# Attention on TensorE: the turning products of the older odd tile moved up behind the even tile's logits

## The chip, the cores and the metric

The kernel runs on one core of one Trainium2 chip. The metric is the device time of one execution in microseconds (us); the time before is the median of three executions. One further execution was profiled, and all rows below come from it.

## The reference, cut to what matters

Input x is 4 x 1024 x 256. Three stages follow one another: a half feed-forward stage, attention, and a half feed-forward stage again. The change touches attention alone, which for each of 4 batches and 16 heads computes

```
dots = einsum('bhid,bhjd->bhij', l2norm(q), l2norm(k)) * 10      # 1024 queries, 1024 + 4 keys
dots = einsum('hg,bgij->bhij', W_pre_th, dots)                   # heads mixed
dots = where(causal, -max, dots)
dots = where(dots < 64th largest of the row, -max, dots)
attn = softmax(dots)
attn = einsum('hg,bgij->bhij', W_post_th, attn)                  # heads mixed again
out  = einsum('bhij,bhjd->bhid', attn, v) * head_scale
x    = x + (out * sigmoid(x @ Wg + bg)) @ Wo
```

## The kernel before

**Tiles, steps, blocks.** Attention works on tiles g of 8 query rows x 16 heads = 128 partitions. There are NT = 512 tiles, 128 for each batch, and they are processed in pairs: step k takes the tiles 2k (even) and 2k+1 (odd), so there are S = 256 steps. Eight steps are a block of 128 query rows. Block ib (0 to 7) of a batch has up to 4 + 128 (ib+1) keys to look at, so all vector work of a tile grows with ib, and the costs of a step too.

**Each engine has its own list of instructions, written out by hand as a loop over k.** The engines meet only at semaphores, and an engine that waits holds up all that stands behind it in its list. What belongs to one tile is spread over several steps (the tile's age is k minus its own step):

- TensorE `units(G, slots[i])`: raw scores of the *next* block, in units of two matmuls (two heads) into banks 0 and 1. There is one pair of banks, so each unit first waits for VectorE's copy of the unit before it (`s_sb`). VectorE's `scored` (line 1372, Sn) copies them out, and a DMA stores them. A step of the first six of a block has four places for units, `slots[0]` to `slots[3]`. Where the next block needs 8 units (and in the last block of all, which has none) `slots[0]` is always empty; with 16 units (blocks 2 to 5) `slots[0]` holds one unit in the steps k%8 = 1, 2, 4, 5; with 24 (block 6) in k%8 = 0 to 5. That makes 22 steps per batch and 88 in all.
- TensorE `mix(g, ..)` (lines 1020, 1024): the mixed logits of tile g, of age 0. VectorE's `take` (line 1383, D) brings them to SBUF. After the odd take GpSimd computes a first guess of the threshold (line 1217, nt), and ScalarE counts against it (line 1142), four rounds over the next steps. TensorE puts two tiny matmuls (lines 1033, 1034) of an older pair behind the odd mix; VectorE reads them as a flag (line 1379) ahead of the odd take.
- VectorE `sides` (line 1397, W), `closest` (1404), `picked` (1412) and `select` (1462, E) find the exact threshold and apply it. `sides` needs GpSimd's line 1252.
- TensorE `post(g)` (line 1047): the **turning products**. One product for each 128 keys turns the probabilities E to keys x (heads, rows) and mixes the heads on the way (its moving operand is kr, line 1285 of GpSimd). Up to four chunks share a bank, two banks take turns, and with more than four chunks a tile has two groups. Even tiles are turned at age 4 at the end of a step, odd tiles at age 5. ScalarE's `turned` (line 1165, AT) evicts them, and a group waits for the eviction of the group two before it (`at`).
- TensorE `values(hb, part)` (lines 1075, 1080): the product with V for 64 query rows, in four parts: part 0 at k%4 = 0, parts 1 and 2 at k%4 = 1, part 3 at k%4 = 2. Part 0 waits for the evictions of its eight tiles. So 64 steps, two in each block (k%8 = 1 and 5), hold part 1; here they are called values steps.

**Order in a step.** VectorE: even take, scored(slots[0]), sides x2, flag, odd take, scored(slots[1]), closest x2, threshold, picked, scored(slots[2]), even select, gated, scored(slots[3]), odd select. ScalarE: last count x2, even turned, second count x2, even exps, odd turned, odd exps, third count x2, first count x2. For values steps TensorE has: even mix, values part 1, unit, odd turning products, odd mix, unit, values part 2, unit, even turning products, unit.

Of the kernel before, what the change touches and what calls it, by code (L numbers as in the profile page):

```python
# [720 lines left out]
S = NT // 2  # L721
# [25 lines left out]
def mix_plan(g):  # L747

    cuts = mix_cuts(g)
    if len(cuts) == 1:  # L750
        return [(0, g % 3)]
    if len(cuts) == 2:
        return [(1, 2), (0, 1)] if g % 2 else [(0, 0), (1, 1)]
    return list(enumerate(range(3)))


def turn_groups(g):

    ib, t = g // TPB % IB, g % TPB
    chunks = list(range(ib + 2 if t == TPB - 1 else ib + 1))  # L760
    return [chunks[i:i + 4] for i in range(0, len(chunks), 4)]
# [12 lines left out]
def unit_slots(G):  # L774

    total = len(score_units(G))
    used = 16 if total <= HP else UNITS
    return [range(total * min(i, used) // used, total * min(i + 1, used) // used) for i in range(UNITS)]
# [5 lines left out]
                post=1, at=1, av=1, ut=1, y=1, x_ok=1, link=1, chain=1, general=1)  # L784


def attention(nc, banks, mkT, kT_all, tail, qd, kd, gd, vd, x1d, x2d, sd, mix_rows, mem_v, Wo_d, delta_c,
# [16 lines left out]
    for G in range(NB):  # L804
        UC.append(UC[-1] + (len(score_units(G)) if G else 0))

    USED = [bank for g in range(NT) for _, bank in mix_plan(g)]
    LAST = [max([j for j in range(max(0, m - 4), m) if USED[j] == USED[m]], default=-1) for m in range(MC[NT])]

    def last_use(m):  # L810

        return LAST[m]

    def searched(p):

        return 0 <= p < S and 2 * p % (IB * TPB) >= FIRST
# [8 lines left out]
    with ExitStack() as ctx:  # L825
# [167 lines left out]
        def _(pe):  # L993
            def units(G, us):
                for u in us:
                    i = UC[G] + u
                    p, (c0, c1) = score_units(G)[u]
                    if u == 0:
                        pe.wait_ge(s["k_in"][G % 2], 16 * (G // 2 + 1))
                        if G == 1:  # L1000
                            pe.wait_ge(s["k_in"][0], 16)
                        pe.wait_ge(s["q_in"], 16 * G)
                        pe.wait_ge(s["kmean"], G + 1)
                    if i >= 1:
                        pe.wait_ge(s["s_sb"], i)
                    nc.tensor.matmul(ps[0][:, 0:c1 - c0], qT[0:DH, p, :], kT[0:DH, p, c0:c1], start=True, stop=True)  # L1006
                    nc.tensor.matmul(ps[1][:, 0:c1 - c0], qT[DH:P, p, :], kT[DH:P, p, c0:c1], start=True,  # L1007
                                     stop=True).then_inc(s["s_ps"], 1)

            def mix(g, p):  # L1010
                pe.wait_ge(s["sg_in"][g % 3], 16 * (g // 3 + 1))
                for i, (k, v) in enumerate(mix_plan(g)):
                    c0, c1 = MP[g][k]
                    m, c, bank = MC[g] + i, c1 - c0, ps[2 + v]
                    diagonal = k == len(MP[g]) - 1
                    if last_use(m) >= 0:
                        pe.wait_ge(s["taken"], TAKE[last_use(m)])
                    if last_use(m) in FLAGGED:
                        pe.wait_ge(s["flag"], FLAGGED[last_use(m)])
                    out = nc.tensor.matmul(bank[:, 0:c], kpre[:].rearrange("p h r -> p (h r)"), Sg[:, g % 3, c0:c1],  # L1020
                                           start=True, stop=not diagonal)
                    if diagonal:
                        pad = len(MP[g]) == 2
                        out = nc.tensor.matmul(bank[:, c - R8 - pad:c], deltab[:], maskb[:, 0:R8 + pad], start=False,  # L1024
                                               stop=True)
                    if m in FLAGGED:
                        out = missed(p, bank)
                    out.then_inc(s["mixed"], 1)

            def missed(p, bank):  # L1030
                e = 2 * p % 8
                pe.wait_ge(s["bad"], FP[p] + 1)
                nc.tensor.matmul(bank[:, HELD:HELD + 1], onesb[:], bad[:, e:e + 1], start=True, stop=False)
                return nc.tensor.matmul(bank[:, HELD:HELD + 1], onesb[:], bad[:, e + 1:e + 2], start=False,
                                        stop=True)

            def post(g):
                pe.wait_ge(s["prob"], g + 1)
                pe.wait_ge(s["kr"], g + 1)
                ib = g // TPB % IB  # L1040
                for j, chunks in enumerate(turn_groups(g)):
                    i = PC[g] + j
                    if i >= 2:
                        pe.wait_ge(s["at"], i - 1)
                    for c in chunks:
                        rows = P if c <= ib else MEM
                        out = nc.tensor.matmul(ps[5 + i % 2][0:rows, c % 4 * P:(c % 4 + 1) * P],  # L1047
                                               E[:, g % 4, c * P:c * P + rows], kr[:, g % 4, :], start=True, stop=True)
                    out.then_inc(s["post"], 1)
# [36 lines left out]
            def project(G):  # L1086
                pe.wait_ge(s["ut"], UT[2 * (G + 1)])
                for p in range(HP):
                    out = nc.tensor.matmul(ps[7][:, 0:DIM], gT[:, p, :], Wo[:, p, :], start=(p == 0),
                                           stop=(p == HP - 1))  # L1090
                out.then_inc(s["y"], 1)
# [3 lines left out]
            for k in range(S + 16):  # L1095
                G = k // 8 + 1
                slots = [range(0)] * 4
                if G < NB and k % 8 < UNITS // 4:
                    slots = unit_slots(G)[4 * (k % 8):4 * (k % 8) + 4]
                if k < S:  # L1100
                    mix(2 * k, k - 3)
                if k >= 9 and (k - 9) % 4 == 0 and (k - 9) // 4 < 2 * NB:
                    values((k - 9) // 4, 1)
                units(G, slots[0])
                if 0 <= k - 5 < S:
                    post(2 * (k - 5) + 1)
                if k < S:
                    mix(2 * k + 1, k - 3)
                elif searched(k - 3):
                    if k == S:  # L1110
                        pe.wait_ge(s["taken"], TC[NT])
                    else:
                        pe.wait_ge(s["flag"], FP[k - 3])
                    missed(k - 3, ps[2]).then_inc(s["mixed"], 1)
                units(G, slots[1])
                if k >= 10 and (k - 10) % 4 == 0 and (k - 10) // 4 < 2 * NB:
                    values((k - 10) // 4, 3)
                if k >= 9 and (k - 9) % 4 == 0 and (k - 9) // 4 < 2 * NB:
                    values((k - 9) // 4, 2)
                if k >= 8 and (k - 8) % 4 == 0 and (k - 8) // 4 < 2 * NB:  # L1120
                    values((k - 8) // 4, 0)
                units(G, slots[2])
                if k >= 15 and (k - 15) % 8 == 0 and (k - 15) // 8 < NB:
                    project((k - 15) // 8)
                if 0 <= k - 4 < S:
                    post(2 * (k - 4))
                units(G, slots[3])
# [708 lines left out]
```

## Time and profile before

| | |
|---|---|
| median of 3 executions | 3582.88 us (3573.04 to 3583.82) |
| the profiled execution | 3581.46 us |
| its span, first to last instruction | 3578.9 us |
| mean granted TensorE clock | 0.943 of full |
| busy, share of the span | TensorE 88%, VectorE 71%, ScalarE 71%, GpSimd 56% |

Attention fills roughly the stretch from 850 to 3330 us. In the timeline rows the first number is the start after the beginning of the span and the next number the length; "x14" means that 14 neighbouring instructions of one form are merged in the row. An fp32 matmul of the kernel shows as two records, and matmuls overlap a little, so a matmul row's length reaches past the start of what follows; the distance from one row's start to the next row's start is what the work takes. In brackets stands how long the engine was idle just before, and who released it. PE is TensorE, DVE VectorE, ACT ScalarE, POOL GpSimd.

### The profile page before, as it was taken

What the parts mean: (1) busy time and instruction counts of PE and PEld (TensorE: products, weight loads), DVE (VectorE), ACT (ScalarE), POOL (GpSimd) and SP (SyncE); (2) the same over time, 40 slices, a digit from 0 to 9 for tenths busy, and PEclk for the clock granted to TensorE, in tenths of its full rate; (3) what the DMA queues carried; (4) which work ended last, traced back from release to release, by engine and by line L of the source; (5) the groups of instructions that cost most, each with busy time, mean ns of one, the idle gap of its engine ahead of it and who ended that gap; (6) DMA issues with size and microseconds to landing.
All of it is one profiled execution on the core that took longest, in us unless ns stands there. A gap on an engine that the chain in (4) does not pass through costs nothing. (4 is left out here: it accounts for less than half of the span.)

```text
span 3578.9 us, 73640 instructions
## 1 busy us (share of the span) xinstructions
PE 3160.2 (88%) x23206; PEld 2089.0 (58%) x23206; DVE 2552.0 (71%) x6406; ACT 2523.4 (71%) x5857; POOL 2016.8 (56%) x6011
## 2 busy tenths in 40 slices
PE   7999999996788998888899887899988889988998
PEld 4444444443556666656666665566676566667566
DVE  4444444444788998678998867899986889986354
ACT  3444454443788999688999967889986888896222
POOL 1221221223787767687776767776777877674332
PEclk9999999996799999989999989999997999999899
DMA  3222222225466664355666345666534556642010
GB/s 129 94 90 104 106 106 94 83 82 173 141 179 179 185 181 98 108 155 173 185 183 157 90 119 151 179 179 186 144 88 130 166 178 181 181 108 74 12 36 30
DMA packets 363531, 467.11 MB, mean 131 GB/s; under 512 B 29476, under 2 KB 295204, under 8 KB 362664
## 3 DMA queue, kind: packets, MB, share of 16 engines
q1 hardware_dynamic: 363048, 461.62, 43.8%
q8 instruction: 187, 3.06, 0.4%
q14 instruction: 296, 2.42, 0.2%
HBM read 227.18 MB, written 234.36 MB: 129 GB/s over the span
## 5 line engine op out<-in xcount | busy, mean ns | idle before, releaser
L1142 ACT ACTIVATE junk<-D,nt 128x76 int8<-128x76 f32 (+62 forms) x1440 | 1070.4, 747 | 98.9 <-POOL nt L1230 65.2
L1047 PE MATMUL banks<-kr,E 128*128 128x128 f32 (+1 forms) x4672 | 707.0, 300 | 106.4 <-ACT AT L1165 60.7
L1047 PEld LDWEIGHTS banks<-kr,E 128*128 128x128 f32 (+1 forms) x4672 | 605.6, 203 | 256.7 <-issue 154.2
L1020 PE MATMUL banks<-Sg,kpre 128*128 128x109 f32 (+51 forms) x1568 | 605.1, 494 | 22.9 <-POOL maskb L1299 13.0
L1372 DVE COPY Sn<-banks 128x686 f32<-128x686 f32 (+11 forms) x440 | 375.5, 853 | 176.2 <-PE banks L1007 145.0
L1397 DVE SCALAR_TENSOR_TENSOR W<-SG,sgn,W 128x76 f32<-128x76 int8 (+14 forms) x480 | 412.8, 899 | 103.4 <-POOL W L1252 102.9
L1006 PE MATMUL banks<-kT,qT 64*128 64x343 f32 (+11 forms) x880 | 395.8, 532 | 101.9 <-DVE Sn L1372 95.9
L1165 ACT ACTIVATE AT<-banks 128x512 f32<-128x512 f32 (+3 forms) x768 | 345.2, 479 | 195.6 <-PE banks L1047 194.5
L1075 PE MATMUL banks<-AT,V 128*64 128x64 f32 x9216 | 394.1, 233 | 87.6 <-issue 75.4
L1075 PEld LDWEIGHTS banks<-AT,V 128*64 128x64 f32 x9216 | 324.2, 143 | 162.6 <-issue 143.1
L1462 DVE SCALAR_TENSOR_TENSOR E<-D,vk,E 128x12 f32<-128x12 f32 (+56 forms) x512 | 394.8, 780 | 3.1 <-ACT E L1152 1.5
L1007 PE MATMUL banks<-kT,qT 64*128 64x343 f32 (+11 forms) x880 | 396.2, 533 | 0.0
L1142 ACT ACTIVATE SG<-D,nt 128x76 int8<-128x76 f32 (+14 forms) x480 | 357.1, 746 | 49.1 <-DVE hit L1412 46.2
L1152 ACT ACTIVATE E<-D,least 128x12 f32<-128x12 f32 (+56 forms) x512 | 369.4, 722 | 9.6 <-POOL E L1279 6.5
L1252 POOL TENSOR_SCALAR W<-D,sgn 128x76 f32<-128x76 f32 (+14 forms) x480 | 375.5, 792 | 0.4
L1383 DVE TENSOR_SCALAR_CACHE_REDUCE D<-banks 128x13 f32<-128x13 f32 (+62 forms) x504 | 339.1, 673 | 41.3 <-PE banks L1024 40.9
L1020 PEld LDWEIGHTS banks<-Sg,kpre 128*128 128x128 f32 x1568 | 267.5, 205 | 169.6 <-issue 114.5
L1404 DVE MAX8 m<-W 128x8 f32<-128x76 f32 (+14 forms) x480 | 326.7, 720 | 22.1 <-issue 19.9
L541 POOL TENSOR_TENSOR a_g2T<-a_gT 128x512 f32<-128x512 f32 x64 | 70.7, 1109 | 460.3 <-ACT a_gT L455 460.3
L1229 POOL TENSOR_TENSOR move<-cnt,tab 128x2 f32<-128x2 f32 x720 | 223.7, 311 | 188.2 <-ACT junk L1142 183.5
L1142 ACT ACTIVATION_READ_ACCUMULATOR junk<-D,nt 128x1 f32 x1440 | 276.0, 192 | 0.0
L1230 POOL TENSOR_TENSOR nt<-move,base 128x2 f32<-128x2 f32 x720 | 224.7, 312 | 56.4
(197 smaller groups left out, 5253.9 us busy)
## 6 DMA issues: line engine op xcount, KB each, us to landing
score_scratch<-Sn SPq DMA_DIRECT2D x96, 343.0 KB, 3.3
v_scratch<-a_share SPq DMA_DIRECT2D x32, 512.0 KB, 3.6
q_scratch<-a_share SPq DMA_DIRECT2D x32, 512.0 KB, 2.8
k_scratch<-a_share SPq DMA_DIRECT2D x32, 512.0 KB, 2.8
gate_scratch<-a_share SPq DMA_DIRECT2D x32, 512.0 KB, 2.7
kT<-k_scratch SPq DMA_DIRECT2D x32, 512.0 KB, 5.0
gateT<-gate_scratch SPq DMA_DIRECT2D x32, 512.0 KB, 10.2
qT<-q_scratch SPq DMA_DIRECT2D x31, 512.0 KB, 6.4
```

What stands on the lines that cost most here:

```text
L1006: nc.tensor.matmul(ps[0][:, 0:c1 - c0], qT[0:DH, p, :], kT[0:DH, p, c0:c1], start=True, stop=True)
L1007: nc.tensor.matmul(ps[1][:, 0:c1 - c0], qT[DH:P, p, :], kT[DH:P, p, c0:c1], start=True, stop=True).then_inc(s["s_ps"], 1)
L1020: out = nc.tensor.matmul(bank[:, 0:c], kpre[:].rearrange("p h r -> p (h r)"), Sg[:, g % 3, c0:c1], start=True, stop=not diagonal)
L1047: out = nc.tensor.matmul(ps[5 + i % 2][0:rows, c % 4 * P:(c % 4 + 1) * P], E[:, g % 4, c * P:c * P + rows], kr[:, g % 4, :], start=True, s ...
L1075: out = nc.tensor.matmul(into, V[:, c, h * DH:(h + 1) * DH], rows, start=(c == 0), stop=(c == ib and (ib > 0 or hb % 2 == 0)))
L1142: nc.scalar.activation(out, D[:, e, 1:1 + n], ACT.Sign, bias=nt[:, r, e:e + 1], scale=-1.0, accum_out=cnt[:, r, e:e + 1]).then_inc(s[f"cnt ...
L1152: nc.scalar.activation(E[:, g % 4, 0:n], D[:, e, 1:1 + n], ACT.Exp, bias=least[:, e:e + 1], scale=-1.0).then_inc(s["exp"], 1)
L1165: out = nc.scalar.activation(AT[:, c0:c0 + c, :, g % RING * R8:(g % RING + 1) * R8], bank[:, 0:c * P].rearrange("p (c h r) -> p c h r", h= ...
L1252: ts(W[:, g % 2, 0:n], D[:, g % 8, 1:1 + n], sgn[:, g % 8:g % 8 + 1], -SMALL, ALU.mult, ALU.mult).then_inc(s["v"], 1)
L1372: nc.vector.tensor_copy(Sn[:, i % 2, :, 0:c1 - c0], banks[:, 0:2, 0:c1 - c0]).then_inc(s["s_sb"], 1)
L1397: nc.vector.scalar_tensor_tensor(out=W[:, h, 0:n], in0=SG[:, h, 0:n], scalar=sgn[:, e:e + 1], in1=W[:, h, 0:n], op0=ALU.is_equal, op1=ALU. ...
L1462: nc.vector.scalar_tensor_tensor(out=E[:, g % 4, 0:n], in0=D[:, g % 8, 1:1 + n], scalar=vk[:, g % 8:g % 8 + 1], in1=E[:, g % 4, 0:n], op0= ...
```

## The change

In each step `post(2 * (k - 5) + 1)`, the turning products of the odd tile of age 5, now stands directly behind the even tile's mix, ahead of values part 1 and of the unit of `slots[0]`. It stood behind both. Nothing is added or removed, and no other engine's list changes.

```diff
                 if k < S:
                     mix(2 * k, k - 3)
+                if 0 <= k - 5 < S:
+                    post(2 * (k - 5) + 1)
                 if k >= 9 and (k - 9) % 4 == 0 and (k - 9) // 4 < 2 * NB:
                     values((k - 9) // 4, 1)
                 units(G, slots[0])
-                if 0 <= k - 5 < S:
-                    post(2 * (k - 5) + 1)
                 if k < S:
                     mix(2 * k + 1, k - 3)
```

## Rows read from the trace of the kernel before

**Rows 1.** Windows, steps 106, 108, 117: busy PE, PEld, DVE, ACT, POOL, clock, DMA

```profile
1769.53:1780.66 11.13, 9.62 (x86) 6.12 (x84) 11.06 (x25) 10.75 (x25) 8.68 (x24) 1.00 0.52 153
1791.50:1802.71 11.21, 11.21 (x97) 7.10 (x96) 10.10 (x23) 9.82 (x23) 8.41 (x24) 0.98 0.62 194
1899.67:1914.09 14.42, 14.42 (x170) 10.13 (x168) 11.87 (x23) 11.85 (x24) 7.15 (x25) 1.00 0.56 166
```

**Rows 2.** Timeline of TensorE in step 117 (block 6, a values step)

```profile
1901.22 0.17 PE L1024 MATMUL banks<-maskb,deltab 128*128 128x9 bf16 x1
...
1903.99 0.45 PE L1007 MATMUL banks<-kT,qT 64*128 64x343 f32 x1
1904.37 1.83 PE L1047 MATMUL banks<-kr,E 128*128 128x128 f32 x14
1906.04 0.90 PE L1020 MATMUL banks<-Sg,kpre 128*128 128x435 f32 x2
```

**Rows 3.** Timeline of VectorE in step 117

```profile
1901.83 1.03 DVE L1383 TENSOR_SCALAR_CACHE_REDUCE D<-banks 128x862 f32<-128x862 f32 x1
...
1904.56 0.87 DVE L1372 COPY Sn<-banks 128x686 f32<-128x686 f32 x1 [1.69 <-PE banks L1007]
1905.35 2.07 DVE L1397 SCALAR_TENSOR_TENSOR W<-SG,sgn,W 128x828 f32<-128x828 int8 x2
1907.84 0.15 DVE L1379 CAST flag<-banks 1x1 int32<-1x1 f32 x1 [0.42 <-PE banks L1034]
1907.91 1.04 DVE L1383 TENSOR_SCALAR_CACHE_REDUCE D<-banks 128x870 f32<-128x870 f32 x1
```

**Rows 4.** Timeline of GpSimd in step 117

```profile
1900.68 2.71 POOL L1252 TENSOR_SCALAR W<-D,sgn 128x828 f32<-128x828 f32 x2
...
1909.05 0.19 POOL L1217 TENSOR_TENSOR nt<-D,tab 128x2 f32<-128x2 f32 x1 [4.23 <-DVE D L1383]
```

**Rows 5.** Timeline of ScalarE in step 117

```profile
1905.57 1.16 ACT L1165 ACTIVATE AT<-banks 128x512 f32<-128x512 f32 x2 [2.19 <-PE banks L1047]
...
1909.46 1.00 ACT L1142 ACTIVATE junk<-D,nt 128x860 int8<-128x860 f32 x1
```

**Rows 6.** Timeline of TensorE, steps 89 (block 3), 105 (block 5)

```profile
1617.01 0.94 PE L1047 MATMUL banks<-kr,E 128*128 128x128 f32 x6
1617.78 0.87 PE L1020 MATMUL banks<-Sg,kpre 128*128 128x421 f32 x2
...
1762.39 1.38 PE L1047 MATMUL banks<-kr,E 128*128 128x128 f32 x10
1763.61 0.74 PE L1020 MATMUL banks<-Sg,kpre 128*128 128x339 f32 x2
```

**Rows 7.** Timeline of TensorE and VectorE in step 108 (block 5)

```profile
1793.58 0.54 PE L1007 MATMUL banks<-kT,qT 64*128 64x450 f32 x1
1794.04 1.69 PE L1047 MATMUL banks<-kr,E 128*128 128x128 f32 x12
...
1794.03 0.08 DVE L1383 DVE_READ_ACCUMULATOR D<-banks 128x1 f32 x1
```

**Rows 8.** Timeline of TensorE and VectorE in step 98 (block 4)

```profile
1692.98 0.17 PE L1024 MATMUL banks<-maskb,deltab 128*128 128x9 bf16 x1
1693.72 0.59 PE L1006 MATMUL banks<-kT,qT 64*128 64x387 f32 x1 [0.57 <-DVE Sn L1372]
...
1694.57 1.16 PE L1047 MATMUL banks<-kr,E 128*128 128x128 f32 x8
...
1695.08 0.96 DVE L1372 COPY Sn<-banks 128x774 f32<-128x774 f32 x1
```

**Rows 9.** Timeline of TensorE and ScalarE in step 121 (block 7)

```profile
1948.40 0.17 PE L1024 MATMUL banks<-maskb,deltab 128*128 128x9 bf16 x1
...
1948.93 0.96 ACT L1165 ACTIVATE AT<-banks 128x512 f32<-128x512 f32 x2
```

**Rows 10.** Waits of the whole span: us, times, longest

```profile
ACT AT L1165 <- PE banks L1047: 194.5, 149, 5.3
```

## The prediction

> **What bounds the kernel now.** I read the page first, for the shares: no engine is full over the span (TensorE is at 88%, VectorE and ScalarE at 71%), so the bound has to be looked for inside a step. The windows over single steps show it. In step 117, a values step, TensorE is busy for all of its 14.42 us while VectorE and ScalarE have some 2.5 us to spare; in step 106 VectorE works for 11.06 of 11.13 us and TensorE has 1.5 us to spare; step 108, which has values part 0 behind the odd mix, shows TensorE full and VectorE with 1.1 us idle [rows 1]. So the bound changes hands: TensorE has it in the steps k%4 = 0 and 1, VectorE and ScalarE have it in the two after, and at each handover the last result of one is what the others start from.
>
> Then the timelines of step 117. TensorE finishes the even mix at 1901.39, does values part 1, then the unit (its second half ends at 1904.44), then the odd turning products from 1904.37 to 1906.04, then the odd mix [rows 2]. VectorE has ended its even take at about 1902.9 and sits idle for 1.69 us until the unit is there; only behind that copy come both `sides`, the flag and the odd take [rows 3]. GpSimd makes the first guess right after the odd take, having idled 4.23 us for it [rows 4], and ScalarE reaches the count of this guess at 1909.46, when it had been ready since 1909.24 (1909.05 + 0.19) [rows 4, 5]. On the same engine the odd eviction waited 2.19 us for the odd turning products [rows 5]. So two ways lead to the first count and they arrive 0.2 us apart: unit, copy, sides, odd take, guess; and odd turning products, eviction, exps, third count. The change makes the second way shorter and the first one longer.
>
> **The change part by part.** No instruction is added, so TensorE's work is the same; only what stands in front of what changes. Between even mix and odd mix nothing is moved out or in, so the odd mix is not earlier. It costs something only where the moved products pass something: the unit of slots[0] (88 steps) or values part 1 (64 steps), 40 steps having both. In the other 144 steps the list is the same as before. No DMA issue is moved; the store of the unit's scores follows its copy and becomes late with it, for a block that starts steps later.
>
> *Can the products run that early?* They need the odd tile's probabilities and kr, which lie in VectorE's list two steps and in GpSimd's list one step back, so both are there. They also need the bank of the group two before. In step 117 the even eviction is done before the even mix is, and no wait arises.
>
> *Length of what is moved.* 6 records take 0.77 us from their start to the odd mix (1617.01 to 1617.78) and 10 take 1.22 [rows 6]; 14 take 1.67 [rows 2]. That is 0.1125 us a record and 0.1 on top. A values step of block ib turns ib chunks at k%8 = 1 and ib+1 at k%8 = 5, two records each.
>
> *Values steps with a unit (blocks 2 to 6, 10 in each batch, 40).* The records of one batch are 4+6+8+10+12 and 6+8+10+12+14, together 90, so 90 x 0.1125 + 10 x 0.1 = 11.1 us, and 44 us over four batches. VectorE already waits for the unit there (1.69 us in row 1904.56), so each of these microseconds comes on top of its wait. What takes some of it up again: a wait of 0.42 us before the flag in step 117 [rows 3], and the 0.2 us by which the first count comes after its guess. The flag's wait is seen in the largest tiles, so I take 0.3 us a step, 12 us. That leaves 32 us. The ends are 44 (nothing taken up) and 40 x (1.1 - 0.62) = 19 us.
>
> By the Trainium skill (Perfetto Trace Analysis, "Tensor Engine Instruction"), ScalarE, VectorE and GpSimd run strictly first in, first out, which speaks against this change. The trace agrees: `sides` had its operands at 1903.39 (1900.68 + 2.71) and yet starts at 1905.35, behind the copy [rows 3, 4]. If VectorE could pass the waiting copy, this term would be about 0 and not 32.
>
> *Steps with a unit and no values part 1 (48).* Here VectorE's even take covers TensorE's unit, and the question is whether it also covers the turning products. Bounds from two steps. In step 108 the unit ends at 1794.12, the take's last record at 1794.11: no cover, and the copy would be late by the full 1.6 us (the products' 12 records) [rows 7]. In step 98 TensorE waited 0.57 us for the copy of the unit before it; the products could use that time (1693.15 to 1694.15), the unit would end at 1695.1 and the copy, which started at 1695.08, is not late at all [rows 8]. Half of these steps, 24, have k%4 = 0, where values part 0 follows and VectorE idles 1.1 us in the step anyway (11.21 less 10.10 in row 1791.50) [rows 1]: I take 0 there; without this cover they cost 24 x 1.6 = 38. The other 24 have VectorE full, as step 106, so a late copy is paid in full; but as there VectorE is the slower of the two, TensorE is ahead as in step 98. Between 0 and 1.6 us I take 0.45, nearer the row of step 98: 11 us.
>
> *Values steps of block 7 (8) and of blocks 0 and 1 (16).* No unit is passed. In block 7 TensorE finishes the even mix at 1948.57, when the two even evictions have just begun (1948.93 to 1949.89) [rows 9], so the products wait there for about 1 us with values part 1 queued behind them, and the odd mix becomes late by as much. ScalarE is the full engine of that block, and its first count does not sit right on its guess there; I take 0, with 8 x 1.3 = 10 us as the other end. In blocks 0 and 1 the odd eviction is earlier but the count is gated by the guess; 16 x 0.2 = 3 us are gained at most, and I take 1.
>
> *Sum.* 32 + 11 + 0 - 1 = 42 us. The profiled execution took 3581.46 us (span 3578.9), 1.4 less than the median; with the change it would take 3623.5, and the median 3625.
>
> **The rivals.**
>
> *Hidden (12%).* VectorE's later copies are caught up because it and ScalarE idle 1 to 2.5 us in the steps k%4 = 0 and 1. For it speaks that 64 of the 88 units passed lie in such steps. Against it: in step 117 the idle time lies before the unit, where it doesn't help, and what follows is packed but for 0.42 us [rows 3]. It would leave the 11 us of the other steps at most and give 3583 to 3593.
>
> *Faster (9%).* ScalarE waited 194.5 us for turning products in all [rows 10], 2.19 of it in step 117. If the late unit didn't matter and the odd eviction were what holds the step, each values step would win back the eviction's wait, up to about 64 x 1.3 = 83 us taking a mean below the 2.19 of the largest tiles: 3500. It is decided by the first count: as soon as the guess is what it waits for, earlier evictions give nothing, and by 1909.24 against 1909.46 this is after 0.2 us, which makes the gain 64 x 0.2 = 13 us: 3570. I hold 3570 for the likely size of this case.
>
> *Slower, but by the wait of block 7 too (within the main case).* If TensorE's new wait counts in full, 10 us are added: 3635.
>
> *The clock.* The granted clock is 0.98 to 1.00 in the three steps [rows 1]. TensorE's own work is unchanged and the new wait is about 1 us in 8 steps, so I give it nothing.
>
> **How the numbers follow.** A measurement here can tell about 0.3%, 11 us. Slower by the sum above, 3600 to 3655, has 72%; a small remainder of it, 3594 to 3600 (both terms mostly taken up), 7%; no change 12%; faster 9%. So slower 0.79, same 0.12, faster 0.09. The low end of the range goes into the hidden case, 3588; the high end takes 44 us for the first term, 15 for the second and 10 for block 7: 3582.9 + 69, rounded to 3652.
>
> **What the profile of the changed kernel would show.** Right: in values steps ScalarE's wait before the odd eviction is gone; VectorE's wait before the first copy grows by the length of the products (step 117: 1.69 to about 3.4 us); the odd take and the first guess come 1 us later after the even mix, and ScalarE now waits for the guess (nt, line 1217) before its first count. The total of VectorE's waits before Sn grows by some 50 us. Wrong: if ScalarE's new wait for the guess stays below 0.2 us a step, or if TensorE's idle time doesn't grow although its work is the same. The prediction fails if the steps k%4 = 0 and 1 are longer paths on TensorE than I think, so that VectorE's lateness is waited out; or if VectorE starts the copy late anyway in most steps, as in step 98.

## The result and the profile after

The changed kernel takes 3635.6 us (median of 4, 3630.1 to 3643.3) against 3578.0 us of the kernel before in the same comparison; the ratio of the two is 1.0184, with a 95% interval of 1.0157 to 1.0211. By the ratio that is 66 us slower (0.0184 x 3578; the interval is some 56 to 75), where 42 us were forecast. The two medians are 58 us apart; the text goes by the ratios here as in the experiments. The profiled execution took 3643.3 us, its span is 3640.9 us. The page after:

```profile
PE 3164.8 (87%) x23206; PEld 2088.1 (57%) x23206; DVE 2540.1 (70%) x6406; ACT 2527.1 (69%) x5857; POOL 1997.2 (55%) x6011
```

The counts are the same and the busy times almost so, as it must be when only an order changes. Nearly all of the 62 us between the spans are waiting, on every engine: TensorE is busy 4.6 us longer (3160.2 before), ScalarE 3.7 (2523.4), VectorE and GpSimd a little less. The waits name it. First five rows of the kernel before, then the same pairs after with the one of [rows 10] (engine, line, who released it, us in total, times, longest):

```profile
DVE Sn L1372 <- PE banks L1007: 145.0, 130, 4.5
POOL nt L1217 <- DVE D L1383: 139.6, 100, 4.6
PE banks L1006 <- DVE Sn L1372: 95.9, 90, 2.5
PE banks L1047 <- ACT AT L1165: 60.7, 39, 3.5
ACT junk L1142 <- POOL nt L1217: 30.3, 48, 13.7
```

```profile
POOL nt L1217 <- DVE D L1383: 222.2, 112, 5.3
DVE Sn L1372 <- PE banks L1007: 210.3, 145, 4.6
ACT junk L1142 <- POOL nt L1217: 155.5, 137, 13.7
ACT AT L1165 <- PE banks L1047: 121.4, 96, 5.2
PE banks L1006 <- DVE Sn L1372: 120.3, 128, 2.8
PE banks L1047 <- ACT AT L1165: 91.6, 60, 3.6
```

VectorE waits 65 us longer for units. ScalarE waits 73 us less for turning products (194.5 in [rows 10]), which is what the new order gives it, and 125 us more for the first guess: it gets to the same place earlier and stands there. TensorE itself waits 31 us more for evictions and 24 us more for VectorE's copy of the unit before, together 55 of the 57 us by which its idle time grows.

Step 117 shows the chain. TensorE, the same stretch as [rows 2]; the products now stand directly behind the even mix:

```profile
1934.97 0.17 PE L1024 MATMUL banks<-maskb,deltab 128*128 128x9 bf16 x1
1934.99 1.81 PE L1047 MATMUL banks<-kr,E 128*128 128x128 f32 x14
1936.73 0.34 PE L1075 MATMUL banks<-AT,V 128*64 128x64 f32 x4
...
1939.40 0.45 PE L1007 MATMUL banks<-kT,qT 64*128 64x343 f32 x1
1939.78 1.00 PE L1020 MATMUL banks<-Sg,kpre 128*128 128x435 f32 x2
```

VectorE, as [rows 3]:

```profile
1935.56 1.03 DVE L1383 TENSOR_SCALAR_CACHE_REDUCE D<-banks 128x862 f32<-128x862 f32 x1
...
1939.97 0.87 DVE L1372 COPY Sn<-banks 128x686 f32<-128x686 f32 x1 [3.37 <-PE banks L1007]
1940.76 2.07 DVE L1397 SCALAR_TENSOR_TENSOR W<-SG,sgn,W 128x828 f32<-128x828 int8 x2
1942.74 0.14 DVE L1379 CAST flag<-banks 1x1 int32<-1x1 f32 x1
1942.81 1.04 DVE L1383 TENSOR_SCALAR_CACHE_REDUCE D<-banks 128x870 f32<-128x870 f32 x1
```

GpSimd, as [rows 4], and ScalarE, as [rows 5]:

```profile
1934.57 2.64 POOL L1252 TENSOR_SCALAR W<-D,sgn 128x828 f32<-128x828 f32 x2
...
1943.95 0.19 POOL L1217 TENSOR_TENSOR nt<-D,tab 128x2 f32<-128x2 f32 x1 [5.30 <-DVE D L1383]
```

```profile
1937.16 0.96 ACT L1165 ACTIVATE AT<-banks 128x512 f32<-128x512 f32 x2
...
1944.17 1.01 ACT L1142 ACTIVATE junk<-D,nt 128x860 int8<-128x860 f32 x1 [3.22 <-POOL nt L1217]
```

Read against before: the wait for the unit was 1.69 us and is 3.37, longer by 1.68, which is the length of the 14 records. The 0.42 us before the flag are gone. From the end of the even mix (1935.14) to the guess (1944.14) it takes 9.00 us; it took 7.85 (1901.39 to 1909.24), so 1.15 more. The odd eviction has no wait any more, but ScalarE then waits 3.22 us at the first count.

The Trainium skill (Perfetto Trace Analysis, "Tensor Engine Instruction") has it that VectorE is strictly first in, first out. Here `sides` had its operands at 1937.21 and started at 1940.76, so the trace agrees.

A second item shows in other steps, and the forecast had it at nothing there. In step 65, the first values step of block 0, the odd tile still belongs to block 7 of the batch before and has two large groups. TensorE before:

```profile
1442.98 0.17 PE L1024 MATMUL banks<-maskb,deltab 128*128 128x8 bf16 x1
1443.08 2.08 PE L1075 MATMUL banks<-AT,V 128*64 128x64 f32 x64
1446.11 2.02 PE L1047 MATMUL banks<-kr,E 128*128 128x128 f32 x16 [0.94 <-ACT AT L1165]
```

and after:

```profile
1460.95 0.17 PE L1024 MATMUL banks<-maskb,deltab 128*128 128x8 bf16 x1
1463.88 3.06 PE L1047 MATMUL banks<-kr,E 128*128 128x128 f32 x16 [2.76 <-ACT AT L1165]
1466.87 2.61 PE L1075 MATMUL banks<-AT,V 128*64 128x64 f32 x64
```

The eviction is what both wait for. Before, values part 1 filled two thirds of the wait; after, TensorE stands idle for 2.76 us and has the values still to do. The windows over steps 65 and 129 (length, busy us of PE, PEld, DVE, ACT, POOL, then clock, DMA share, GB/s) before:

```profile
1442.74:1454.47 11.73, 9.90 (x178) 8.84 (x176) 9.46 (x22) 7.59 (x13) 8.74 (x15) 1.00 0.16 45
2046.06:2057.55 11.49, 9.90 (x178) 8.83 (x177) 9.22 (x21) 7.60 (x13) 8.56 (x14) 1.00 0.16 47
```

and after:

```profile
1460.60:1474.98 14.38, 11.62 (x178) 10.37 (x176) 11.47 (x28) 7.61 (x12) 9.42 (x16) 0.88 0.15 44
2081.88:2096.25 14.37, 11.62 (x178) 10.37 (x176) 11.46 (x28) 7.61 (x12) 9.42 (x16) 0.88 0.15 44
```

Each is 2.7 to 2.9 us longer. Not all of this is the wait. The same 178 records keep TensorE busy for 11.62 us instead of 9.90, because the granted clock fell to 0.88 in these steps. Step 193, the third of this kind, shows the new wait without a lower clock:

```profile
2702.48 0.17 PE L1024 MATMUL banks<-maskb,deltab 128*128 128x8 bf16 x1
2705.37 2.02 PE L1047 MATMUL banks<-kr,E 128*128 128x128 f32 x16 [2.72 <-ACT AT L1165]
```

It is only 1.3 us longer than before (12.77 us at clock 1.00 against 11.47). And the step behind is 0.9 us shorter in all three places, so that each pair of steps loses 1.8, 2.0 and 0.4 us.

A wait for the eviction, with a unit behind it, stands in step 106 too (TensorE, then VectorE):

```profile
1799.19 0.17 PE L1024 MATMUL banks<-maskb,deltab 128*128 128x9 bf16 x1
1801.19 1.35 PE L1047 MATMUL banks<-kr,E 128*128 128x128 f32 x10 [1.83 <-ACT AT L1165]
1802.47 1.06 PE L1006 MATMUL banks<-kT,qT 64*128 64x451 f32 x1
```

```profile
1804.40 1.10 DVE L1372 COPY Sn<-banks 128x902 f32<-128x902 f32 x1 [2.03 <-PE banks L1007]
```

Here VectorE, which before was full in this step (11.06 of 11.13 us, [rows 1]), waits 2.03 us for the unit. The step takes 14.20 us instead of 11.13; 1.8 us of this is a longer busy time of TensorE (11.43 against 9.62 us), again at a clock of 0.88.

### The profile page after: what moved, and what is told of

It reads as the page before. It is cut to its first block and busy times, and to the rows that moved or that the text cites. A ratio compares the mean times of both kernels' runs of the same rounds, so it can differ in the third digit from the quotient of the medians.

```text
span 3640.9 us, 73640 instructions
## 1 busy us (share of the span) xinstructions
PE 3164.8 (87%) x23206; PEld 2088.1 (57%) x23206; DVE 2540.1 (70%) x6406; ACT 2527.1 (69%) x5857; POOL 1997.2 (55%) x6011
## 3 DMA queue, kind: packets, MB, share of 16 engines
q8 instruction: 187, 3.06, 0.4%
## 5 line engine op out<-in xcount | busy, mean ns | idle before, releaser
L1047 PE MATMUL banks<-kr,E 128*128 128x128 f32 (+1 forms) x4672 | 700.6, 298 | 142.3 <-ACT AT L1165 91.6
L1020 PE MATMUL banks<-Sg,kpre 128*128 128x109 f32 (+51 forms) x1568 | 614.8, 500 | 22.1 <-POOL maskb L1299 13.1
L1006 PE MATMUL banks<-kT,qT 64*128 64x343 f32 (+11 forms) x880 | 391.7, 527 | 127.3 <-DVE Sn L1372 120.3
L1007 PE MATMUL banks<-kT,qT 64*128 64x343 f32 (+11 forms) x880 | 392.0, 527 | 0.0
```

## The experiments

All were timed in five rounds against the kernel before. "Us" is the ratio less 1, times the 3571 us of before.

| kernel | ratio to before | 95% interval | us |
|---|---|---|---|
| values_steps_only | 1.0139 | 1.0116 to 1.0163 | +50 |
| other_steps_only | 1.0035 | 1.0023 to 1.0048 | +12 |
| pass_unit_only | 1.0180 | 1.0156 to 1.0205 | +64 |
| blocks_7_0_1_only | 1.0030 | 1.0013 to 1.0048 | +11 |
| block_7_only | 1.0013 | 1.0003 to 1.0023 | +5 |
| no_slot0_before | 1.0328 | 1.0306 to 1.0351 | +117 |
| no_slot0_after | 1.0329 | 1.0305 to 1.0353 | +117 |
| unit_first | 0.9989 | 0.9974 to 1.0005 | -4 |
| unit_post_values | 1.0038 | 1.0023 to 1.0053 | +14 |
| values_behind_mix | 0.9970 | 0.9957 to 0.9983 | -11 |
| values_behind_unit1 | 0.9935 | 0.9918 to 0.9951 | -23 |
| values_behind_unit2 | 0.9924 | 0.9909 to 0.9939 | -27 |

**Where is it paid?** Two kernels share the change out: one makes it at k%4 = 1 alone, the other in all other steps.

```diff
+                if 0 <= k - 5 < S and k % 4 == 1:      # values_steps_only; other_steps_only has != here
+                    post(2 * (k - 5) + 1)
                 ...
-                if 0 <= k - 5 < S:
+                if 0 <= k - 5 < S and k % 4 != 1:      # and == here
                     post(2 * (k - 5) + 1)
```

> The moved order in the 64 values steps alone; all others as before. Theory A (the late unit in slots[0] delays VectorE's copy, the sides, the odd take and the first guess, and it is paid where TensorE is the bound): most of the change's 65 us, so 45 to 58 us slower than before. Rival B (the other steps, where VectorE is full, carry it): under 20 us slower.

> The moved order in the 48 steps that have a unit in slots[0] and no values part 1. Theory A: 5 to 15 us slower, as VectorE's even take covers part of the products and later waits the rest. Rival B: 40 us slower or more.

Measured: +50 and +12 us, together 62 of the 66. So four fifths lie in the values steps, where TensorE is the bound, as expected.

**Is it the unit, or values part 1, that mustn't be passed?** First the products ahead of the unit only, in all steps; then the moved order in the blocks without a unit in slots[0].

```diff
                     values((k - 9) // 4, 1)
-                units(G, slots[0])
                 if 0 <= k - 5 < S:
                     post(2 * (k - 5) + 1)
+                units(G, slots[0])
```

> Turning products ahead of the unit, but behind values part 1, in all steps. Theory A: the unit is as late as with the full change, so blocks 2 to 6 lose the same, 45 to 55 us slower; what the full change costs beyond that (5 to 12 us) belongs to blocks 7, 0 and 1, where no unit is passed. Rival C (it is values part 1, held up behind the products' wait for an eviction, that costs): under 20 us slower.

```diff
+                if 0 <= k - 5 < S and k // 8 % 8 in (7, 0, 1):
+                    post(2 * (k - 5) + 1)
                 ...
-                if 0 <= k - 5 < S:
+                if 0 <= k - 5 < S and k // 8 % 8 not in (7, 0, 1):
                     post(2 * (k - 5) + 1)
```

> The moved order in blocks 7, 0 and 1 alone, where slots[0] is empty and only values part 1 is passed. Theory A with the new wait for the eviction as a second, smaller item: 5 to 12 us slower, with three steps (the first values steps of block 0 behind a block 7) some 2.5 us longer each. If blocks 2 to 6 carry all: within 4 us of before. Rival C: over 30 us slower.

Measured: +64 and +11. Passing the unit alone costs as much as the whole change, more than the 45 to 55 expected. The two add up to 75, above the 66 of the change; their intervals are some 9 and 6 us to a side, so the remainder of 9 can't be read as anything. In the steps without values part 1 this kernel has the same list as the change, so the eviction's wait of step 106 is in the 64 us too.

Then the unit was taken away from the place: slots[0] is empty on all engines and slots[1] holds both.

```diff
-    return [range(total * min(i, used) // used, total * min(i + 1, used) // used) for i in range(UNITS)]
+    cut = [total * min(i, used) // used for i in range(UNITS + 1)]
+    return [range(cut[i - (i % 4 == 1)], cut[i + (i % 4 > 0)]) for i in range(UNITS)]
```

> Order of the kernel before, with the unit of slots[0] moved to slots[1] on all engines, so that slots[0] is empty everywhere. It is the base for the next kernel. Against before it may be some 10 to 40 us slower, since two units then stand in one place, each waiting for a copy; no theory hangs on that.

> The changed order with slots[0] empty everywhere. Theory A (the cost is the unit that becomes late): against no_slot0_before at most 12 us slower, what blocks 7, 0 and 1 cost by themselves. Rival C (values part 1 held up by the products, whatever the unit does): still 45 us slower or more.

The base itself is 117 us slower than before, three times the top of what I had allowed: two units in one place, each waiting for the copy of the one ahead, are dear. TensorE's wait for copies grew from 95.9 to 168.1 us, and its busy time by 31 us (3160.2 to 3191.2) for the same instructions, at a mean clock of 0.933 instead of 0.943. On this base the changed order costs nothing that could be measured: 1.0328 against 1.0329, 3689.6 against 3692.6 us. The difference has some 12 us to a side, so the 11 us of blocks 7, 0 and 1 may well be in it, but a loss of 50 us is ruled out. The waits of the two traces (their executions are 22 us apart, more than the medians) show that ScalarE's gain and loss are there all the same. No_slot0_before, then no_slot0_after (lines are one higher there):

```profile
ACT AT L1166 <- PE banks L1048: 187.1, 157, 4.2
DVE Sn L1373 <- PE banks L1008: 182.9, 171, 4.6
...
ACT junk L1143 <- POOL nt L1218: 33.1, 58, 13.7
```

```profile
DVE Sn L1373 <- PE banks L1008: 192.6, 172, 5.3
ACT AT L1166 <- PE banks L1048: 142.5, 125, 5.2
...
ACT junk L1143 <- POOL nt L1218: 77.3, 102, 14.8
```

ScalarE waits 45 us less for products and 44 us more for the guess, which balances; VectorE's wait for units grows by 10 us, not 65. With the unit gone from behind the products the loss is gone. One reservation stays: this base is held up elsewhere for 117 us, and that its own waits hide a part of the loss is not excluded. The direct proof is pass_unit_only, on the base of the kernel before.

**The wait for the eviction.**

```diff
+                if 0 <= k - 5 < S and k // 8 % 8 == 7:
+                    post(2 * (k - 5) + 1)
                 ...
-                if 0 <= k - 5 < S:
+                if 0 <= k - 5 < S and k // 8 % 8 != 7:
                     post(2 * (k - 5) + 1)
```

> The moved order in the 8 values steps of block 7 alone, where the products wait for the even eviction with values part 1 behind them. If TensorE's wait is made good in the steps after (the traces show these 8 steps longer and the next ones shorter by as much): within 4 us of before. If it counts in full: 10 us slower. What is missing from the 11 us of blocks_7_0_1_only is then the cost of blocks 0 and 1, of the first values step behind a block 7 above all.

Measured: +5 us, between the two, with an interval of 1 to 8. In its trace the wait is made good in part: step 121 takes 13.2 us instead of 11.4, step 122 then 10.2 instead of 11.3. The difference to the 11 us of all three blocks would leave some 6 for blocks 0 and 1; its interval is some 7 us to a side, so this is a hint and not a result. The two traces with blocks 0 in the new order point the same way: in the changed kernel and in blocks_7_0_1_only the first three steps of block 0 (64 to 66, 128 to 130, 192 to 194) are longer by 7 us in all, the clock's share included, against 1 us in block_7_only.

**Both orders of the unit against the values.** The unit ahead of values part 1, with the products behind (unit_first: units, values, post) or between (unit_post_values: units, post, values).

> In the 40 values steps with a unit, the unit ahead of values part 1, products behind both: even mix, unit, values, products, odd mix. Theory A: VectorE's copy and sides come 1 to 2 us earlier, but the odd take still needs the odd mix, which is not earlier, and ScalarE's way by the odd eviction stays 0.2 us behind the guess; 0 to 10 us faster. If the unit alone set the step: 30 us faster.

> In values steps: even mix, unit, products, values part 1, odd mix. The products pass values part 1 but no unit; the unit passes values too. Theory A: both ways to the first count are shorter and only the odd mix gates it: 2 to 20 us faster than before, less 5 to 10 for the waits in blocks 7 and 0, so between 12 us faster and 5 us slower. Rival C: slower by over 20 us, as the products are ahead of values just as in the change.

Measured: -4 us with an interval that includes zero, and +14. An earlier copy alone gives nothing measurable, as the odd mix gates the odd take: in the trace of unit_first VectorE waits 50 us less for units (95.0), but 38 us more for the flag, which stands behind the odd mix (58.3 us against 20.4), and ScalarE's wait for the guess is unchanged (30.6). Products ahead of values cost 14 us even with no unit behind them; 11 of that is what blocks 7, 0 and 1 cost. The second is outside what I wrote (5 us slower at most): I had put the waits of blocks 7 and 0 at 5 to 10 us and counted on a gain of at least 2 besides.

**Values part 1 behind the odd mix.** If the first guess is what the next steps wait for, values part 1 is the one that stands wrong: it needs nobody's answer and holds up the odd mix. Order: even mix, unit, products, odd mix, then values part 1 at once (values_behind_mix), behind the unit of slots[1] (values_behind_unit1), or behind part 2 and the unit of slots[2] (values_behind_unit2).

```diff
-                if k >= 9 and (k - 9) % 4 == 0 and (k - 9) // 4 < 2 * NB:
-                    values((k - 9) // 4, 1)
                 units(G, slots[0])
                 ...
                 units(G, slots[1])
+                if k >= 9 and (k - 9) % 4 == 0 and (k - 9) // 4 < 2 * NB:
+                    values((k - 9) // 4, 1)      # values_behind_unit1
```

> In values steps: even mix, unit, odd products, odd mix, values part 1, unit, values part 2. Theory A says that the odd mix gates the odd take and the first guess. With values part 1 behind it, these come 1 to 2 us earlier in 64 steps, while the unit of slots[1], and with it VectorE's next copy, comes as much later. If the first guess is what the next steps wait for: 10 to 40 us faster than before. If VectorE's order (the second copy ahead of closest and picked) decides: 0 to 20 us slower.

> As values_behind_mix, but values part 1 stands behind the unit of slots[1] too, directly ahead of part 2. No copy of slots[0] or slots[1] waits behind values; only the unit of slots[2] stands behind both parts. If each unit that is late holds VectorE: better than values_behind_mix in the middle of the step and worse at slots[2]; from 40 us faster to 20 us slower than before, and faster than values_behind_mix.

> In values steps, values part 1 behind part 2 and the unit of slots[2]; behind it only the even products and the last unit. If it is only late units that cost: 5 to 15 us faster than values_behind_unit1 (about 30 to 40 us faster than before). If the even products, whose eviction ScalarE does early in the next step, are then the late item: no better than values_behind_unit1, or up to 20 us slower than it.

Measured: -11, -23 and -27 us; the last two can't be told apart, so the 5 to 15 us that values_behind_unit2 was to gain over values_behind_unit1 were not seen. Whether the even products took them back, as the expectation has it, stays open. Step 117 of values_behind_unit1 (VectorE, ScalarE, GpSimd):

```profile
1893.08 0.87 DVE L1372 COPY Sn<-banks 128x686 f32<-128x686 f32 x1
1893.87 2.07 DVE L1397 SCALAR_TENSOR_TENSOR W<-SG,sgn,W 128x828 f32<-128x828 int8 x2
...
1895.94 1.04 DVE L1383 TENSOR_SCALAR_CACHE_REDUCE D<-banks 128x870 f32<-128x870 f32 x1
...
1901.89 0.87 DVE L1372 COPY Sn<-banks 128x686 f32<-128x686 f32 x1 [1.73 <-PE banks L1007]
```

```profile
1897.48 1.00 ACT L1142 ACTIVATE junk<-D,nt 128x860 int8<-128x860 f32 x1
```

```profile
1897.07 0.19 POOL L1217 TENSOR_TENSOR nt<-D,tab 128x2 f32<-128x2 f32 x1 [0.23 <-DVE D L1383]
```

The copy follows the even take with no idle time, and the even mix, which ended at 1891.69 in that trace, is followed by the guess after 5.57 us (1897.26) instead of 7.85. Not all of this is kept: VectorE's wait comes back as 1.73 us before the unit of slots[2], which now stands behind both parts.

## Why the prediction was right, and by how much it was short

The direction and the mechanism were right, the size was two thirds of what was measured (42 of 66 us; 42 of 58 by the medians). The signs that it named came in step 117 and in the totals: VectorE's wait before the first copy 3.37 us (about 3.4 was said), the guess 1.15 us later (1), VectorE's waits for units 65 us longer (some 50). By its own steps:

- *TensorE's work is unchanged, the odd mix is not earlier.* Right: equal counts and busy times, and in step 117 from the even mix's end to the odd mix's start 4.65 us before (1901.39 to 1906.04) and 4.64 after (1935.14 to 1939.78).
- *Values steps with a unit, 32 us.* The mechanism was shown in step 117: VectorE's wait grew by exactly the products' length. Of these 1.67 us 0.5 were made good before the guess and another 0.2 before the first count (1909.46 less 1901.39 is 8.07 us, 1944.17 less 1935.14 is 9.03), so 0.7, where I had taken 0.62 at the most and 0.3 on average. Measured are the 50 us of values_steps_only less the 11 of blocks 7, 0 and 1, so 39, between my 32 and my upper end of 44. The difference of the two has an interval of some 10 us to a side, so this term cannot be called mis-sized. The traces put the truth nearer the upper end, and say why. Added up over the timeline rows of these 40 steps, VectorE's waits before copies grew from 55.0 to 93.8 us, while its waits before the flag, which were to take part of this up, had been only 2.6 us in all. From even mix to even mix these steps are 37 us longer together. The 12 us that I took off were read from step 117, which is one of the largest tiles.
- *The other steps with a unit, 11 us.* Measured 12. No kernel measured the halves apart, but step lengths in the traces (even mix to even mix) do: the 24 steps with k%4 = 0 are 2.4 us longer together, in the changed kernel and in other_steps_only alike, where I had 0; the other 24 are 21 and 12.5 us longer, of which the steps directly behind them give back 7, where I had 11. The way of it was not only the one I gave: in step 106 the new wait of 1.83 us for an eviction made the unit later still.
- *Blocks 7, 0 and 1, -1 us.* This is the term that was wrong: +11. I took 0 for block 7, with 10 as the other end, and 5 was measured (1 to 8). For blocks 0 and 1 I looked for a gain at the first count and overlooked that the first values step of block 0 turns a tile of block 7, whose two groups wait for evictions. The cover was values part 1, and it was moved behind the wait. That this is where the rest of the 11 us lies is likely by the step lengths, but not shown by a kernel of its own.
- *The bank is free, no wait arises.* Said from step 117, and true there; wrong as a general statement: TensorE's waits for evictions before turning products went from 60.7 to 91.6 us. With the new order in blocks 7, 0 and 1 alone it is 77.3, in the other steps with a unit alone 72.1, in the values steps alone 65.1. One step was taken for all.
- *The clock, nothing.* Right for the whole, where TensorE's busy time grew by 4.6 us. In steps 65, 106 and 129 it was 1.7 to 1.8 us each, which the sum did not foresee.
- *The rival "faster".* Its gate was named rightly: ScalarE won 73 us at the evictions and lost 125 at the guess.
- *The rival "hidden".* Not so; no_slot0_after suggests what it would have needed: no unit behind the products.

My terms as measured, 39 + 12 + 11, give 62 of the 66 us; the rest is within the intervals. Left open is what share of the 39 and 12 is the new wait for evictions with a unit behind it and what the products' length alone; no kernel took that wait away by itself.

## What to carry to other kernels

When several engines meet in each step, look for the result that the slowest part of the *next* stage starts from, and keep work off its way that nobody waits for soon. Moving work ahead so that one engine stops waiting gives nothing if that engine has a second, later gate; and the work that it passes may be the head of a longer chain on an engine that takes its list in order. Before a waiting instruction is moved up, check its wait in all phases of the loop, the seams between blocks and batches above all, because what stood ahead of it was its cover.

## What the runs showed of the hardware that was not expected

After some of the new waits TensorE's granted clock fell for a moment. Windows of the changed kernel in step 106, around the wait of 1.83 us (length, busy times, then the clock as third number from the end):

```profile
1801.20:1802.50 1.30, 1.30 (x12) 1.18 (x12) 1.14 (x5) 1.30 (x4) 1.14 (x5) 1.00 0.78 281
1802.50:1804.30 1.80, 1.80 (x6) 0.50 (x5) 0.00 (x0) 1.80 (x6) 1.72 (x5) 0.52 1.00 228
```

In the second of them the clock was at its lower level, 1.2 GHz, nearly throughout, and a unit's matmul took 1.06 us where the same one took 0.64 before the change. In step 65, after 2.76 us of idle time, 16 records of turning products took 3.06 us instead of 2.02. Over the whole of these two steps TensorE was busy 1.8 and 1.7 us longer for the same records, on top of the wait. It isn't general. In step 193 a wait of 2.72 us stood in the same place, and the clock stayed at 1.00: the same 16 records took 2.02 us. The kernel before has such stretches too: its clock is 0.87 over step 107, in which TensorE waits 2.24 us for VectorE's copy. The mean clock is 0.946 after and 0.943 before, and TensorE's busy time as a whole grew by 4.6 us, so the clock explains little of the 66 us. What decides whether such a wait costs the clock is not shown here.
